# Softmax attention on one core: maxima of two score tiles in one VectorE instruction, two PSUM banks for scores, one for small products

## What is computed

```python
q, k, v = heads of layernorm(x) @ w_qkv          # 8 batches, 16 heads, 8 features, 512 tokens
attn = softmax(einsum('bhnd,bhmd->bhnm', q, k) / sqrt(8))
y = einsum('bhnm,bhmd->bhnd', attn, v) @ w_proj
```

## Time and profile before

| | us |
|---|---|
| median of 3 runs | 692.49 (689.46 to 693.12) |
| the profiled execution | 689.38 |
| its span, first to last instruction | 687.6 |
| softmax groups 0 to 3 | about 53 |
| softmax groups 4 to 29 | about 279 |
| softmax groups 30 and 31 | about 10, and the start of the last stretch |

### The profile page before, as it was taken

How to read it: one execution, slowest core, us unless ns; L and a number is a source line. 1 busy time by engine, 2 the same in 40 slices (tenths; PEclk the granted TensorE clock), 3 DMA queues, 4 the chain that set the end, 5 groups by cost and what they waited for, 6 DMA issues and landing times.

```text
span 687.6 us, 16368 instructions
## 1 busy us (share of the span) xinstructions
PE 610.6 (89%) x5305; PEld 304.8 (44%) x5305; DVE 590.7 (86%) x1489; ACT 500.5 (73%) x1071; POOL 411.6 (60%) x922
## 2 busy tenths in 40 slices
PE   4689789988877788999999999999999999899994
PEld 2456456655544222222333332333323322589993
DVE  6878999998877988899999999999999994775552
ACT  3545677787655387888888888888888889765661
POOL 4213558667656642436676887877877862566553
PEclk9899999999999699999999999999999999999997
DMA  6564234335364121137110301203012010556510
GB/s 181 161 229 131 66 107 135 120 116 185 113 165 139 48 92 47 47 107 231 49 47 2 116 25 53 77 13 116 25 52 78 13 48 23 139 174 174 167 33 9
DMA packets 42899, 66.25 MB, mean 96 GB/s; under 512 B 7948, under 2 KB 36335, under 8 KB 39808
## 3 DMA queue, kind: packets, MB, share of 16 engines
q1 hardware_dynamic: 39232, 56.73, 27.9%
q0 software_dynamic: 3296, 8.41, 3.4%
q10 hardware_dynamic: 288, 0.07, 0.0%
HBM read 41.64 MB, written 22.26 MB: 93 GB/s over the span
## 4 chain that ended last, share of the span: by engine, by line
PE 53%; ACT 18%; DVE 16%; issue 6%; SPq 2%; POOL 2%; DMA 2%; ACTq 0%; POOLq 0%; DVEq 0%
PE bank L1090 12%; ACT arena L2058 11%; PE pair L1079 8%; PE bank L1051 7%; PE pair L1338 4%; DVE arena L1409 4%; DVE arena L1596 3%; PE bank L1101 2%; PE bank L1347 2%; PE pair L1347 2%; PE bank L936 2%; PE pair L1131 2%; DVE fq_all L1573 1%; PE pair L990 1%; PE pair L1051 1%
## 5 line engine op out<-in xcount | busy, mean ns | idle before, releaser
L2058 ACT ACTIVATE arena<-pair 128x512 f32<-128x512 f32 x506 | 278.1, 602 | 52.8 <-PE pair L1079 50.9
L1596 DVE TENSOR_REDUCE arena<-bank 128x1 f32<-128x512 f32 x388 | 251.3, 682 | 10.1 <-PE bank L1051 7.2
L1079 PE MATMUL pair<-q_stack,k_stack 64*128 64x512 bf16 x506 | 158.7, 388 | 5.4 <-ACT arena L2058 4.9
L1051 PE MATMUL bank<-k_stack,q_stack 63*128 63x512 bf16 x388 | 136.0, 394 | 10.3 <-DVE arena L1596 6.0
L1090 PE MATMUL bank<-arena,values 128*9 128x512 f32 x1024 | 134.7, 598 | 1.6 <-ACT arena L2058 1.5
L1409 DVE TENSOR_TENSOR arena<-bank,cst 128x512 f32<-128x512 f32 x128 | 82.0, 681 | 12.8 <-PE bank L922 12.5
L1596 DVE TENSOR_REDUCE arena<-pair 128x1 f32<-128x512 f32 x124 | 84.3, 680 | 2.7 <-PE pair L1051 2.3
L726 POOL TENSOR_TENSOR arena<-arena 128x32 f32<-128x32 f32 (+6 forms) x312 | 68.4, 219 | 24.4
L1051 PEld LDWEIGHTS bank<-k_stack,q_stack 63*128 63x128 bf16 x388 | 33.1, 93 | 110.5 <-ACT arena L2063 25.9
L1079 PEld LDWEIGHTS pair<-q_stack,k_stack 64*128 64x128 bf16 x506 | 40.7, 93 | 47.4 <-ACT arena L2058 23.2
L1051 PE MATMUL pair<-k_stack,q_stack 63*128 63x512 bf16 x124 | 48.8, 393 | 0.7 <-ACT v_all L2083 0.3
(11 more groups left out here) (307 smaller groups left out, 1211.9 us busy)
## 6 DMA issues: line engine op xcount, KB each, us to landing
softmax_parts<-arena SPq DMA_DIRECT2D x8, 768.0 KB
q_stack<-softmax_parts SPq DMA_DIRECT2D x48, 128.0 KB
k_stack<-softmax_parts SPq DMA_DIRECT2D x48, 128.0 KB
linear_parts<-arena SPq DMA_DIRECT2D x7, 768.0 KB, 3.7
q_stack<-linear_parts SPq DMA_DIRECT2D x42, 128.0 KB
k_stack<-linear_parts SPq DMA_DIRECT2D x42, 128.0 KB
arena<-in_L_ffn_w_dram SPq DMA_DIRECT2D x16, 256.0 KB, 5.0
v_all<-token_rows SPq DMA_DIRECT2D x20, 192.5 KB, 2.7
```

The lines of the kernel that those rows point to most:

```text
L1051: pe.matmul(bank[:], qs[b % 2][rows, slot, qt * P:(qt + 1) * P], ks[b % 2][rows, slot, :], start=True, stop=True).then_inc(d_s_m, 1)
L1079: pe.matmul(score_bank(s)[:], ks[u][rows, 2 * g + x, kt * P:(kt + 1) * P], qs[u][rows, 2 * g + x, :], start=True, stop=True).then_inc(d_s_ ...
L1596: dve.reduce_max(mx[:, m % 2, col:col + 1], bank[:], AX).then_inc(d_s_mr, 1)
L2058: act.activation(pt[:, kt % 2, x, half, :], score_bank(s)[:], ACT.Exp, scale=SCALE).then_inc(d_s_e, 1)
```

## The change

The eight banks are allocated as four neighbouring pairs. Maximum tiles now use two pairs alone: tiles 0 and 1 of a step fill one pair, tiles 2 and 3 the other, and DVE reduces a pair of banks, 128 x 2 x 512, in one instruction that writes two columns. `mx`'s semaphore therefore counts pairs (`maxima_of`). The first 32 maxima (groups 0 and 1) stay single. Pieces have a bank of their own (`b_misc`, bank 7), which is taken from the scores: these keep banks 5 and 6, so that a score waits for the exponential two tiles earlier. Groups 30 and 31 use four banks for scores.

PE's order in a step is now: s0, maximum tiles 0 and 1, s1, the piece, s2, maximum tiles 2 and 3, s3, `values` of the step before. DVE's and ACT's small work moves to fit: `d_numerators_out` goes to the front of step 1 (it was behind E2 of step 0), `maxima_out` behind E1 of step 0 (was step 1), `d_output_out` behind E1 of step 2 (was step 3), `d_normalise` behind the second pair of step 1 (was the first tile of step 2).

```diff
-        k.bank = [top.enter_context(nc.psum_tensor(f"bank{i}", [P, 4 * P], F32)) for i in range(4)]
-        k.pair = [top.enter_context(nc.psum_tensor(f"pair{i}", [P, 8 * P], F32)) for i in range(2)]
-        k.bank += [k.pair[0][:, 0:512], k.pair[0][:, 512:1024], k.pair[1][:, 0:512], k.pair[1][:, 512:1024]]
+        k.pair = [top.enter_context(nc.psum_tensor(f"pair{i}", [P, 8 * P], F32)) for i in range(4)]
+        halves = [k.pair[i // 2][:, 512 * (i % 2):512 * (i % 2) + 512] for i in range(8)]
+        k.bank = [halves[i] for i in (0, 1, 6, 2, 3, 4, 5, 7)]
...
-        b_s = [k.bank[5], k.bank[6], k.bank[7]]
+        b_s = [k.bank[5], k.bank[6]]
         b_t = b_s + ring[2:4]
+        b_misc = k.bank[7]
...
+        def piece_bank(n, kt):
+            return ring[kt % 2] if n >= NB - 2 else b_misc
+        def maxima_of(m, pairs):
+            return 16 * m + 2 * pairs if m < 2 else 32 + (m - 2) * 8 + pairs
...
                 def turn_maxima(m, bank):
-                    pe.wait_ge(d_s_mr, m * 16 + 16)
+                    pe.wait_ge(d_s_mr, maxima_of(m, 8))
...
                     elif t < len(b_t):
-                        pe.wait_ge(d_s_mr, NB * 16)
-                        pe.wait_ge(d_s_fh, NB - 2 - G)
+                        pe.wait_ge(d_s_mr, maxima_of(NB, 0))
...
+                def maximum(n, kt, j):
+                    if j % 2 == 0:
+                        pe.wait_ge(d_s_mr, maxima_of(n + 2, 2 * kt + j // 2 - 1))
+                    max_scores(n + 2, 4 * kt + j, k.bank[0:2][j] if j < 2 else k.bank[3:5][j - 2])
+                def turn_maxima_bank(n):
+                    if n == 0:
+                        pe.wait_ge(c_s_r1, 2 * LATE[0])
...
+                    elif n == 2:
                         pe.wait_ge(d_s_gb, 1)
...
+                def step(n, kt):
+                    if n + 2 < NB:
+                        scores(n, kt, 0)
+                        maximum(n, kt, 0)
+                        maximum(n, kt, 1)
+                        scores(n, kt, 1)
+                        piece(n, kt)
+                        scores(n, kt, 2)
+                        maximum(n, kt, 2)
                         maximum(n, kt, 3)
                         scores(n, kt, 3)
...
+                        values_before(n, kt)
+                    else:
+                        for i in range(4):
+                            scores(n, kt, i)
+                        values_before(n, kt)
+                        pe.wait_ge(d_s_mr, maxima_of(NB, 0))
+                        piece(n, kt)
...
+                def maxima(m, kt, i):
+                    col = i * 4 + kt
+                    dve.wait_ge(d_s_m, m * 16 + 4 * kt + 2 * i + 2)
+                    dve.reduce_max(mx[:, m % 2, col:col + 9:8], k.tiles(k.pair[i][:], 2), AX).then_inc(d_s_mr, 1)
...
+                            for i in range(2):
+                                maxima(n + 2, kt, i)
+                                if kt == 1 and n >= G:
+                                    (d_normalise if i else d_denominators)(n - G, piece_bank(n, kt))
+                                if kt == 3 and i == 0 and n >= G:
+                                    add(n - G, piece_bank(n, kt))
...
+                        if kt == 1 and 1 <= n < NB - 2:
+                            d_numerators_out(n - 1)
                         for i in range(4):
                             probs(n, kt, i)
...
+                                if i == 1 and kt == 0:
+                                    maxima_out(n + 1, piece_bank(n, kt))
+                                if i == 1 and kt == 2 and n >= G:
+                                    d_output_out(n - G, piece_bank(n, kt))
```

More of the change, by code:

```diff
@@ L1184, in bank_of_late_piece @@
                         pe.wait_ge(c_s_p1, 2 * LATE[1] + 2)
-                    elif n == 3 and kt == 2:
+                    elif n == 4:
                         pe.wait_ge(c_s_vc, LATE[1] + 1)
[L1188 to L1194, removed]
-                    elif kt == 1:
[L1196 to L1218, removed]
+                    else:
+                        pe.wait_ge(d_s_fh, n - G)
@@ new lines, in piece @@
+                def piece(n, kt):
+                    bank = piece_bank(n, kt)
+                    if kt == 0 and n + 1 < NB:
+                        turn_maxima_bank(n)
+                        turn_maxima(n + 1, bank)
+                    elif kt == 1:
+                        if n + 1 < NB:
+                            pe.wait_ge(d_s_mc, n + 2)
+                        else:
+                            pe.wait_ge(d_s_fh, n - G)
+                        if n == 0:
+                            late_query(LATE[0], bank)
+                        elif n == 1:
+                            gate_shift(bank)
+                        elif n == 2:
+                            late_turn(LATE[1], bank)
+                        elif n == 3:
+                            late_value(LATE[1], bank)
+                        else:
+                            d_turn(n - G, bank)
+                    elif kt == 2:
+                        if n == 0:
+                            pe.wait_ge(c_s_p1, 2 * LATE[0] + 1)
+                            late_key(LATE[0], bank)
+                        elif n == 2:
+                            late_query(LATE[1], bank)
+                        elif n >= G:
+                            d_turn_back(n - G, bank)
+                    elif kt == 3:
+                        if n == 0:
+                            pe.wait_ge(c_s_p1, 2 * LATE[0] + 2)
+                            late_value(LATE[0], bank)
+                        elif n == 2:
+                            pe.wait_ge(c_s_p1, 2 * LATE[1] + 1)
+                            late_key(LATE[1], bank)
+                        elif n >= G:
+                            d_project(n - G, bank)
@@ L1219, in step, with values_before @@
+                def values_before(n, kt):
                     if kt:
@@ L1222, in step @@
                         values(n - 1, C - 1)
-                    if ahead:
+                def step(n, kt):
[7 more added lines that the diff above has]
+                        maximum(n, kt, 2)
                         maximum(n, kt, 3)
                         scores(n, kt, 3)
[L1226 to L1255, removed]
+                        values_before(n, kt)
+                    else:
+                        for i in range(4):
[3 more added lines that the diff above has]
+                        piece(n, kt)
                 pe.wait_ge(w_s_v, SILU)
@@ L1843, in _ @@
                     for kt in range(C):
[L1844 to L1849, removed]
-                                    late_piece(n, kt)
-                                if n >= 10 and n % C == 2 and 4 * kt + j < 7:
-                                    choose((n - 10) // C, 4 * kt + j)
-                        elif n == NB - 2 and kt == 0:
-                            for i in range(7):
-                                choose((n - 10) // C, i)
@@ L2180, in _ @@
                                 late_piece(n, kt, i)
[L2181 to L2186 removed]
+                            if n + 2 >= NB:
+                                if i == 2 and kt == 0:
+                                    d_numerators_out(n - 1)
+                                if i == 1 and kt == 1 and n + 1 < NB:
+                                    maxima_out(n + 1, piece_bank(n, 0))
+                                if i == 1 and kt == 3:
+                                    d_output_out(n - G, piece_bank(n, 2))
+                            else:
+                                if i == 1 and kt == 0:
+                                    maxima_out(n + 1, piece_bank(n, kt))
+                                if i == 1 and kt == 2 and n >= G:
+                                    d_output_out(n - G, piece_bank(n, kt))
                 def weights(j):
```

78 lines of the change are left out of this document (31 added, 47 removed).

## The result

The changed kernel takes 717.85 us (median of 4 runs, 716.7 to 718.47) beside 692.50 us of the kernel before (689.46 to 693.12): a ratio of 1.037, interval 1.0345 to 1.0397. Slower, and 2.9 us above the 715 that were forecast. Its profiled execution took 716.70 us, its span is 714.8 us.

What follows compares the result with a forecast made beforehand. DVE was taken to set the pace, 10.4 of 10.7 us a group. A PE-ACT loop adds 26 us: 689.4 + 26 - 2 + 1 = 714, forecast 715 us, range 705 to 726.

Steps and rivals of the forecast that it cites:

- E1: ACT's exponential of a step's second score tile; its length and the signal to the fourth score: 0.65 us.
- The loop: Each step on PE and ACT: first score, two exponentials, fourth score, `values`, next step's first score, in sequence: 2.885 us.
- the numerators' copy: ACT's `d_numerators_out` waits for the group's last `values`, ahead of step 1's first exponential: 0.17 us a group.
- The pairs: DVE reductions of 1024 elements, 1.22 us each, counting 1.14 instead of 1.20: 0.5 us a group saved, becoming idle time.
- What bounded the kernel before: DVE sets the pace with 10.4 of 10.7 us a group; PE has about 1 us of slack, ACT more.
- The pieces: Pieces on PE, in their own bank, waiting for DVE: up to some 0.3 us late at no cost.
- VectorE keeps pace: Rival: with a step below 2.68 us DVE's saving would count, 674 us in all; chance 0.05.
- the clock falls: Rival: PE's waits ahead of scores lower the clock in one step in four, 738 us; chance 0.06.
- pieces late: Rival: pairs of 1.36 us or pieces 0.2 beyond their cover, either 719 to 720 us, both 725; chance 0.1.
- Groups 0 to 3: Softmax's first groups, 52.2 us: pieces no longer stop the maximum tiles, -2 us, bounds -6 and 0.
- Ahead of the softmax: Stretch before the first exponential of group 0: no change, 0 us.
- the end: Groups 30 and 31 and the rest, with four score banks instead of five: +1 us, at most 2.5.

Runs made afterwards that it cites:

- the first split version: Changed kernel with `values` split into two halves, one behind s1 and one behind s3, and the piece between s0 and s1: 752.75 us, ratio 1.0886.

## Why the prediction was right

**The loop.** The rivals differed in one question: is a step of PE, ACT and PE again longer than 2.68 us? Each term that was read from the kernel before stands beside what the changed kernel shows:

| term | predicted | measured |
|---|---|---|
| s0 to the start of E0 | 0.46 | 0.43 |
| E0 to E1 | 0.485 | 0.49 |
| E1 to s3 | 0.65 | 0.65 |
| s3 to `values` | 0.31 | 0.31 |
| `values` to the next s0 | 0.98 | 0.98 |
| a step | 2.885 | 2.86 |
| the numerators' copy, a group | 0.17 | 0.20 |
| a group | 11.71 | 11.64 |

The last line of what was measured is the sum 4 x 2.86 + 0.20; the turns of the maxima of groups 4 and 29, on PE's timeline, give the same, (585.61 - 294.53) / 25 = 11.64.

```profile
294.53 0.28 PE L1059 MATMUL pair<-cst,arena 128*16 128x128 f32 x1
...
585.61 0.28 PE L1059 MATMUL pair<-cst,arena 128*16 128x128 f32 x1
```

That the sum fits doesn't show that each term is in the loop. The joints of PE and ACT show it: s2 starts within 0.06 us of the end of E0 in 92 of the 104 steps, s3 of the end of E1 in 99. The experiments show it for two terms: shorter exponentials and shorter `values` each brought the time under the kernel before. With short `values` DVE's reductions then hardly wait; with short exponentials PE's own row of starts is nearly the whole step.

**The numerators' copy** ahead of E0 of step 1 showed as expected: ACT's timeline has it begin once `values` is done, with E0 right behind it, 0.63 after its score at 459.81, 0.20 later than in the other steps.

```profile
459.95 0.60 ACT L2075 ACTIVATE fq_all<-pair 128x512 f32<-128x512 f32 x1 [0.39 <-PE pair L1090]
460.44 2.16 ACT L2058 ACTIVATE arena<-pair 128x512 f32<-128x512 f32 x4
```

**The pairs.** 1.22 us was estimated from two sizes, 1.220 is measured. The saving by starts came out as taken: with short `values` three pairs in a row take 3.51 us and follow each other by 1.145, and with the pairs undone six singles in a row take 3.67 and follow each other by 0.60, so a pair saves 0.06.

```profile
323.46 3.51 DVE L1598 TENSOR_REDUCE arena<-pair 128x2 f32<-128x1024 f32 x3
...
337.50 3.67 DVE L1599 TENSOR_REDUCE arena<-pair 128x1 f32<-128x512 f32 x6
```

The group times show less, 0.25 to 0.36 for eight pairs, 0.03 to 0.045 each; where the rest goes is not shown. By the Trainium skill (VectorE: DVE Perf Modes, "The TRN2 errata") merging two PSUM reads would save the fixed 120 cycles, an estimate of 0.125 us. The durations alone, 2 x 0.682 - 1.220 = 0.14, seem to agree, but they overlap in the stream; the starts decide, for half of it. For the forecast none of this mattered, as it said: the gain became idle time, 37.7 us ahead of the reductions.

**What bounded the kernel before** was read too simply. The prediction counts 10.4 us a group for DVE and lets it alone set the pace. With short `values` an ordinary group of the kernel before takes 10.07: the reciprocal counts 0.16 to the next start there, not 0.34, and the addition 0.20, not 0.3.

```profile
336.04 0.25 DVE L1602 RECIPROCAL arena<-bank 128x16 f32<-128x16 f32 x1
336.20 0.63 DVE L1597 TENSOR_REDUCE arena<-bank 128x1 f32<-128x512 f32 x1
```

So about 0.5 of the 10.6 us of an ordinary group were held by `values` on PE, and hardly show as idle time of DVE in the earlier trace rows. The forecast did not suffer, because four steps of 2.86 are longer than either figure.

**The pieces** cost nothing or nearly so, as taken. In step 1 s2 started 0.16 us later than usual in 7 of 26 groups, at no cost; in step 2 it started 0.3 later behind `d_turn_back` in 5, and the step grew by 0.02 to 0.08. That this cover is needed the first split version showed: a piece put too early cost 27 us.

**VectorE keeps pace, the clock falls, pieces late:** none came. DVE is busy 87.5% where about 85% was said; the granted clock of groups 4 to 29 is 1.00, though s3 was held back by 0.26 us in nearly every step (0.49 behind s2, where 0.23 is the distance of two pairs that nothing holds); the long gap of ACT is 0.4 to 0.7, not 0.8.

**Groups 0 to 3: forecast -2, measured 0.0.** The gain named was there: group 1 went from 14.36 to 12.55 us. It was given back: group 3 took 11.72 instead of 11.28, and group 0 took 16.2 instead of 14.75. In the windows the granted clock of group 0 was 0.50 until 243.5 us in the kernel before and about that until 250.3 in the changed one:

```profile
238.90:243.50 4.60, 4.47 (x18) 0.90 (x22) 4.60 (x9) 3.55 (x8) 0.66 (x4) 0.50 0.00 0
...
241.60:246.00 4.40, 3.39 (x13) 0.67 (x12) 3.82 (x5) 2.77 (x6) 0.79 (x4) 0.50 0.00 0
246.00:250.30 4.30, 4.30 (x16) 0.76 (x14) 2.43 (x4) 2.37 (x5) 0.00 (x0) 0.56 0.87 317
```

The first is the kernel before. PE is busy 3.39 of 4.40 us in the first stretch after, 4.47 of 4.60 before; that the sparser start kept the clock low is likely, but no run here varied it alone. The longer group 0 is no accident of this profile: it took 15.85 to 17.6 us in every version with two banks for scores, the kernel before with two banks among them, and 14.1 and 14.75 in the two with three.

**Ahead of the softmax: forecast 0, measured +2.8.** The instructions there are the same. Between the two profiled executions PE waited longer for one DMA, and the granted clock of the stretch that follows (56 to 60 us) was 0.50 instead of 1.00. First the kernel before, then after:

```profile
54.52 0.40 PE L922 MATMUL bank<-q_stack,k_stack 63*128 63x128 bf16 x8 [0.89 <-DMA k_stack<-linear_parts]
56.00:60.00 4.00, 3.72 (x62) 2.72 (x63) 3.12 (x11) 1.81 (x7) 1.16 (x1) 1.00 0.17 55
...
54.83 0.40 PE L925 MATMUL pair<-q_stack,k_stack 63*128 63x128 bf16 x8 [2.33 <-DMA k_stack<-linear_parts]
56.00:60.00 4.00, 3.61 (x36) 2.23 (x32) 1.43 (x3) 2.18 (x6) 1.16 (x1) 0.50 0.01 4
```

The runs of the kernel before spread over 3.7 us, of the same size, and the other profiles say that it is scatter: the first exponential of group 0 came at 238.9, 239.2 and 241.2 us in the three versions with the old order of PE, and between 239.1 and 242.2 in the changed kernel and the seven made from it. Of what the profiled execution lies over the sum of 714, these 2.8 and the 2 us of groups 0 to 3 are above it, 2.2 us of the loop and 0.4 of the end below it. The parts err by 0.4 to 2.8 us and in both directions, so that the total came out within 3 us is in part luck; the loop, which decided, was 2.2 us too long of 26.

## What to carry to other kernels

Before a buffer is taken from a ring between two engines, write down the loop it closes: from the first use to its release, and from there through everything that stands in order ahead of the next use; if the sum of the starts is longer than the present pace, the other engine's gain becomes idle time, however busy that engine is. The terms of such a loop can be read to a few hundredths from the kernel before, long before the loop binds. A saving on the busiest engine is worth something only while nothing else closes at its pace: here the same change is 25 us slower with a long product in the loop, and 8 us faster with a short one.

## What the runs showed of the hardware

One VectorE reduction over two neighbouring PSUM banks (128x1024) takes 1.220 us, two of one bank 0.682 each, but in a stream they start 1.14 and 0.60 apart, so a pair saves 0.06. From the product `values` of 512 columns in four column tiles to the next score it is 0.98 us with float32 operands and 0.33 us when the upper halves of the same words are read as bf16 at a stride of two; with 256 columns of the former it is 0.55, not 0.49. PE's waits of 1.54 us (465.13, changed kernel with short `values`) and 2.33 us (54.83, changed kernel) were followed by stretches at a granted clock of 0.50; a wait of 0.89 (54.52, kernel before) and the 0.26 ahead of s3 in nearly every step were not.
